# Attention kernel on one core: the middle of the long half's weight sums on GpSimd, two later groups on VectorE one step later, and one load moved up

## The reference

```python
Q = split_heads(x, 16)                      # 16 wide per head
K = split_heads(x @ Wk + bk, 16)
V = split_heads(x @ Wv + bv, 16)            # 64 wide per head
attn = softmax(Q @ K^T + causal_mask)
o = merge_heads(attn @ V)
x = layernorm(x + (x + gelu(o) @ Wf + bf))
x = layernorm(x + (x + ffn(x)))             # silu(x wg) * (x wu), then wd
```

## Time and profile before

| what | value |
|---|---|
| median of 3 runs | 1847.62 us (1847.26 to 1853.65) |
| the profiled execution's own time | 1849.75 us |
| its span, first to last instruction | 1848.0 us |
| PE busy | 1762.1 us, 95% of the span |
| DVE busy | 1396.5 us, 76% |
| POOL busy | 1221.8 us, 66% |
| ACT busy | 1050.4 us, 57% |
| mean granted clock of TensorE | 0.991 |

### The profile page before, as it was taken

How to read it: one execution, slowest core, us unless ns; L and a number is a source line. 1 busy time by engine, 2 the same in 40 slices (tenths; PEclk the granted TensorE clock), 3 DMA queues, 4 the chain that set the end, 5 groups by cost and what they waited for, 6 DMA issues and landing times. The chain is left out here.

```text
span 1848.0 us, 37611 instructions
## 1 busy us (share of the span) xinstructions
PE 1762.1 (95%) x10304; PEld 961.4 (52%) x10304; DVE 1396.5 (76%) x3417; ACT 1050.4 (57%) x1375; POOL 1221.8 (66%) x1146
## 2 busy tenths in 40 slices
PE   7999999999999999999999999888889999999996
PEld 5444444444444444444444444333466767676763
DVE  4787877778787787777778787886467878787864
ACT  2465665665565565665666565555545555555552
POOL 3488888888888888888888888999512222222221
PEclk9999999999999999999999999999999999999998
DMA  9675657556565655646556565563477565756500
GB/s 323 160 232 160 181 141 203 161 161 188 142 176 170 168 160 159 195 139 185 169 148 196 145 174 143 144 183 99 138 201 175 172 170 172 169 172 170 171 24 23
DMA packets 261152, 303.16 MB, mean 164 GB/s; under 512 B 28240, under 2 KB 177872, under 8 KB 261072
## 3 DMA queue, kind: packets, MB, share of 16 engines
q1 hardware_dynamic: 261072, 302.19, 58.3%
HBM read 174.20 MB, written 127.93 MB: 163 GB/s over the span
## 5 line engine op out<-in xcount | busy, mean ns | idle before, releaser
L802 POOL TENSOR_TENSOR weight_sum<-weight_sum,weights 128x512 f32<-128x512 f32 (+1 forms) x444 | 731.9, 1649 | 151.9 <-DVE weight_sum L1347 115.3
L1161 ACT ACTIVATE weights<-ring 128x1024 f32<-128x1024 f32 x576 | 570.7, 1026 | 221.2 <-PE ring L846 217.8
L846 PE MATMUL o_acc<-weights,v_pair 128*64 128x512 f32 (+3 forms) x3072 | 586.3, 501 | 17.1 <-POOL weights L757 16.4
L837 POOL TENSOR_TENSOR h_lo<-hidden,h_hi 128x512 f16<-128x512 f32 x96 | 114.4, 1193 | 390.2 <-ACT h_hi L1099 390.2
L1312 DVE TENSOR_REDUCE part_max<-ring 128x2 f32<-128x1024 f32 x256 | 301.0, 1217 | 86.4 <-PE ring L846 86.4
L846 PEld LDWEIGHTS o_acc<-weights,v_pair 128*64 128x64 f32 x3072 | 188.3, 136 | 302.7 <-issue 257.0
L1321 DVE CUSTOM_DVE_ANT_0 scrap<-ring,causal,part_max 128x256 bf16<-128x256 f32 (+3 forms) x512 | 251.3, 547 | 70.7 <-PE ring L846 70.4
L1321 DVE CUSTOM_DVE_ANT_0 scrap<-ring,causal 128x128 bf16<-128x128 f32 (+3 forms) x512 | 225.1, 486 | 91.1 <-PE ring L846 90.6
L846 PE MATMUL ring<-q_stack,k_stack 50*128 50x512 f32 (+3 forms) x1536 | 264.3, 382 | 26.1 <-DVE part_max L1312 17.6
L846 PE MATMUL ring<-k_stack,q_stack 48*128 48x512 f32 (+3 forms) x1536 | 256.9, 373 | 0.1
L846 PE MATMUL ring<-wf_sb,g 128*128 128x256 f32 x1024 | 230.5, 380 | 2.6 <-DVE y_pre L1416 1.7
(11 more groups left out here) (125 smaller groups left out, 2070.1 us busy)
## 6 DMA issues: line engine op xcount, KB each, us to landing
v_pairs<-v_unit SPq DMA_DIRECT2D x64, 512.0 KB, 3.5
v_pair<-v_pairs SPq DMA_DIRECT2D x64, 512.0 KB, 5.1
o_heads<-o_pair SPq DMA_DIRECT2D x64, 512.0 KB, 3.2
g<-o_heads SPq DMA_DIRECT2D x16, 2048.0 KB, 8.1
den_wide<-reciprocals SPq DMA_DIRECT2D x32, 1024.0 KB, 13.3
q_stack<-q_rows SPq DMA_DIRECT2D x128, 192.0 KB, 3.7
k_stack<-k_rows SPq DMA_DIRECT2D x128, 192.0 KB, 4.4
q_rows<-x_hi SPq DMA_DIRECT2D x28, 512.0 KB, 3.6
```

Of the source, the lines that this page charges most:

```text
L802: pool.tensor_tensor(dst, other, weights(t), ALU.add).then_inc(s_add, 1)
L837: pool.tensor_tensor(h_lo[:, f], h32[f % 2][:], h_hi[:, f], ALU.subtract).then_inc(s_hl, 1)
L846: return nc.tensor.matmul(o, l, r, start=start, stop=stop)
L1161: nc.scalar.activation(W[i][:], bank_of("t", i)[:], ACT.Exp).then_inc(s_w, 1)
```

## The change

The two full additions of VectorE and two full additions of GpSimd change places. GpSimd now makes 4 + 5 (`begin_sum`, L788, right behind `add(1)`), + 6, + 10, + 9 and + 11, all within the pair's own step. VectorE makes + 7 and + 8 (`late_sum`, L1353) in bursts 1 and 2 of the next step, each at the head of its burst, and the first waits until GpSimd is through with all of the pair's sums; a new semaphore `s_late` counts them, and `denominators` and the exponentials 6 and 7 wait on it. The order on GpSimd behind the masks of uses 7 and 8 changes with it. Apart from that, `load_x(ALONE, True)` goes directly behind `load_stacks(0, 0)`, and the first `x_high` from burst 3 to burst 0 of step 0.

```diff
-        ADDS = (1, 2, 3, 10, 7, 8, 9, 11)
+        ADDS = (1, 2, 3, 6, 10, 9, 11)
...
             load_stacks(0, 0)
+            load_x(ALONE, True)
             store_early_v(0, 0)
...
             store_early_v(0, 2)
-            load_x(ALONE, True)
             store_early_v(0, 3)
...
+            def begin_sum(rt, n):
+
+                pool.wait_ge(s_w, NU * n + use_of(5) + 1)
+                if rt >= 2:
+
+                    pool.wait_ge(s_den, n - 1)
+                    settle(pool, s_passed["pool"])
+                pool.tensor_tensor(acc1[rt % 2][:], weights(4), weights(5), ALU.add).then_inc(s_add1, 1)
...
                 if now:
                     mask(0, *m)
                     mask(1, *m)
-                if LEAD < r <= PAIRS + LEAD:
-                    add(11, r - LEAD - 1, n - LEAD - 1)
-                if now:
                     mask(2, *m)
                     if r < PAIRS:
-                        for t in (1, 2, 3):
-                            add(t, *m)
+                        add(1, *m)
+                    begin_sum(*m)
                 if r % 4 == 0 and unit_beside(r, it) is not None:
                     x_low(unit_beside(r, it))
                 if now:
+                    if r < PAIRS:
+                        add(2, *m)
+                        add(3, *m)
+                    add(6, *m)
                     add(10, *m)
-                    add(7, *m)
                     mask(7, *m)
-                    add(8, *m)
                     mask(8, *m)
                     add(9, *m)
+                    add(11, *m)
...
                 pe.wait_ge(s_add, NA * (n + 1))
+                pe.wait_ge(s_late, 2 * (n + 1))
...
-                    if b == 3 and r % 4 == 0 and unit_beside(r, it) is not None:
+                    if b == (3 if r else 0) and r % 4 == 0 and unit_beside(r, it) is not None:
                         x_high(unit_beside(r, it), r == 0)
...
+            def late_sum(t, rt, n):
+
+                dve.wait_ge(s_add, NA * (n + 1))
+                if t == 8:
+
+                    dve.wait_ge(s_late, 2 * n + 1)
+                dst = acc1[rt % 2][:, :, BANK - width_of(t):BANK]
+                v.tensor_tensor(dst, dst, weights(t), ALU.add).then_inc(s_late, 1)
...
-                    if b == 4 and LEAD <= r < PAIRS + LEAD:
-                        carry_sum(r - LEAD, n - LEAD)
+                    if b in (1, 2) and LEAD < r <= PAIRS + LEAD:
+                        late_sum(6 + b, r - LEAD - 1, n - LEAD - 1)
                     for what, j in uses(b):
                         if what == "s" and r < PAIRS:
                             top(j, r, n)
...
-                    if b == 2 and LEAD <= r < PAIRS + LEAD:
-                        begin_sum(r - LEAD, n - LEAD)
```

More of the change, by code:

```diff
@@ L292, in build @@
         s_add = sem("sums_made")
+        s_late = sem("late_sums_made")
         s_den = sem("den_ready")
@@ L791, in add @@
                     pool.wait_ge(s_w, NU * n + use_of(t) + 1)
[L792 to L798, removed]
+                if t == 6:
+                    pool.wait_ge(s_add1, n + 1)
+                if t != 1:
                     pool.wait_ge(s_add, NA * n + added(t) - 1)
@@ L1155, in exponent @@
                     act.wait_ge(s_pv, NS * (n - 1) + max(PV_ORDER.index(t) for t in T_USES[i]) + 1)
-                    if i in (3, 4, 5):
-                        act.wait_ge(s_add1, 2 * (n - 1) + (1 if i < 5 else 2))
+                    if i in (3, 4):
+                        act.wait_ge(s_add1, n)
+                    elif i in (use_of(7), use_of(8)):
+                        act.wait_ge(s_late, 2 * (n - 1) + (1 if i == use_of(7) else 2))
                     else:
```

## The result

The changed kernel takes 1932.09 us in the median (1931.63 to 1935.84, 4 runs), against 1848.62 for the kernel before in the same comparison: a ratio of 1.0447, 95% interval 1.043 to 1.0465. The forecast was 1909 in a range of 1870 to 1930. Direction and place were right; the size was short by 23 us and fell 2 us outside the range.

The account below looks back on a forecast made before the run. PE was taken as the bound in steps 3 to 56, GpSimd in the steps without jobs. 1849.75 + 66 + 4 - 5 - 4 = 1910.75, or 1909 us on the median's scale; range 1870 to 1930.

Parts of the forecast that it names:

- The meeting of `late_sum(8)` and `add(1)`: Steps 3 to 56: `late_sum(8)` asks 0.28 us behind GpSimd's `add(1)`, is held off, and ends 1.09 behind it.
- +1.22 per step, +66: Steps 3 to 56: new PE wait of 1.57 us at transposed scores 5, old 0.35 goes; bounds 54 to 81.
- the rival of GpSimd as the bound: Steps 3 to 56: late GpSimd makes `late_sum(7)` and VectorE wait; 0.6 us per step, 32, giving 1875; chance 0.06.
- one of the signs of being wrong: In steps 3 to 56, `late_sum(7)` waiting for GpSimd would show the forecast wrong.
- The clock falls too (0.03): Steps 3 to 56: each wait also lowers the clock, 1.4 us per step, 76 on top, giving 1985; chance 0.03.
- The steps without jobs, +4: Seven GpSimd-bound steps, 57 to 63: late maxima may come round to GpSimd; 0 to 11 us, taken as 4.
- The head, -5: Start: load of x 8.3 us earlier, PE's wait of 4.34 and 1.4 of slower matmuls go; bounds -2 to -6.
- The end, -4: Last pairs: GpSimd's idle before their sums goes, masks 7 and 8 come earlier; bounds 0 to -7.
- the risk that the prediction named: In the head: the next stack load, not moved, is at risk; no size of its own given.

Follow-up runs that it names:

- The cut by head: The changed kernel with GpSimd's `add(1)` cut into two instructions, one per head; 1861.03 us, ratio 1.0048.
- the runs at 0.55 and 0.95: The changed kernel with `add(1)` cut in two: by head (wait 0.55), 1861.03 us; by columns, 288 of 384 first (wait 0.95), 1882.46 us.
- 336 columns first: The changed kernel with `add(1)` cut in two by columns, 336 of 384 in the first instruction; 1899.15 us, ratio 1.0271.
- both additions cut: The changed kernel with `add(1)` and `late_sum(8)` cut by head, the latter's first half in burst 1 behind `late_sum(7)`; 1845.63 us, ratio 0.9971.

## Why the prediction was right on the wait and wrong on the clock

Against the profiled execution the account closes: head -6.0, steps 3 to 56 +85.45, the seven steps +10.1, from there on -3.5; together 86.1, which is 1934.1 less 1848.0.

- **The meeting of `late_sum(8)` and `add(1)`: right.** Asked 0.21 to 0.37 behind in 59 of the 61 steps (0.58 in two), held to the end, 1.08 more each time (forecast 0.28, 1.09). The cut by head shows that the hold is what does it.
- **+1.22 per step, +66: right as the idle time it was, 60.3**, inside the bounds of 54 to 81. The wait was 1.37 in place of 1.57: PE came to the transposed scores 5 at 8.73 us into its step and not at 8.57, and the maxima were ready 0.04 sooner. The step behind `x_low` waits some 0.5 more, because `late_sum(7)` waits 0.96 for GpSimd there. That is the rival of GpSimd as the bound, and one of the signs of being wrong, true in one step of four; I had divided its lateness by four and found it covered, but a lateness that falls in one step is not averaged away.
- **"The clock falls too (0.03)": this is the step that failed.** I dismissed it because the steps without jobs wait in every step at a granted clock of 1.00, and priced it only as all or nothing, 54 dips of 1.4; the sum held nothing for it. It happened in 15 of the 54 steps, 1.6 us each: +25.1. The rows leaned on did not reach as far as the forecast: the waits in that stretch of before are mostly of this size,

```profile
1198.30 1.72 PE L846 MATMUL o_acc<-weights,v_pair 128*64 128x512 f32 x8 [1.23 <-POOL weights L757]
```

  shorter than the 1.57 that I forecast and the 1.37 that came. In the order of the changed kernel, the runs put the change of behaviour between a wait of 1.16 per step, 1 dip, and one of 1.37, 15 dips. That length was what the rows lacked is only in part an explanation: one wait of before, ahead of 1235.04, was 1.52 and brought no dip, and with `late_sum(8)` in burst 1 waits of mostly 1.1 and then 0.39 in one step of four brought 8. The Trainium skill ("TensorE: Matmul & The Clock Gate", section "A second HAM failure mode: psum-queue depth-cycling") says of another kernel that short idles between groups of matmuls, coming often enough, make the clock swing between its two levels. By that rule the trace agrees in 15 of 54 steps, and in the runs at 0.55 and 0.95 it does not.
- **The steps without jobs, +4: mis-sized, +10.1.** The waiting there cost 1.4, inside the bounds; the other 8.7 are the clock again.
- **The head, -5: right (-6.0), shown alone (1843.18 us). The end, -4: -3.5.** `x_hi` is made at 29.43 (forecast 30), and PE waits for no `x_lo`; it waits 1.2 us for the next stack load instead, the risk that the prediction named.

Without the 33.8 us of slower matmuls the changed kernel would, by estimate, stand near 1898 (1932.1 less 33.8), inside the range. The other terms came out some 9 us below the forecast together (60.3, 1.4, -6.0 and -3.5 in place of 66, 4, -5 and -4) and hid that much of the missing one, so it is luck that the time lies only 2 us outside.

## What to carry to other kernels

Price a new wait on TensorE in two parts, its idle time and what the clock may take behind it, and give the second its own partial case: "no dip at 1.2 us per step" says nothing of 1.4. Between VectorE and GpSimd, look at which of two additions asks first; whoever is a few tenths late waits out the other's whole instruction. Here cutting the longer one in two took the kernel from 1932 to 1861 us, and asking before it to 1882, with the same additions on each engine. And work that an engine does in one step of four must find its slack in that step, not in the mean.

## What the runs showed of the hardware that was not expected

- In the order of the changed kernel the dips set in abruptly. From 0.95 to 1.16 us of wait per step they went from 0 to 1, from 1.16 to 1.37 from 1 to 15: busy time rose by another 22 us, for 11 of added idle.
- Which steps dip is not settled, and the length of the wait alone does not settle it. A wait of 1.7 in one step of four, with 0.57 in the others, gave 3 dips; 1.37 in most steps gave 15. In the steps behind an `x_low`, waits of 1.1 (1.5 in three of them) and 0.39 gave a dip in 8 of 13 steps (`late_sum(8)` in burst 1), waits of 0.33 and 1.30 in 1 of 13 (336 columns first). In the seven steps without jobs, 1.1 and 0.4 gave 3 dips with both additions cut, where 1.23 gave none before. Steps 29 and 33 of the changed kernel have the same work and the same waits, and one dips. No run here separates the length of a wait from what PE does before and after it.
- Cutting a GpSimd addition by head adds little work: the first half took 1.00 us, and the second 1.0 in the one case of 62 in which VectorE did not hold it off, against 1.83 for the whole. Held off, the second took 1.99, which GpSimd had to spare here.
